# A language-model tower on one core: a Fourier weight update and a weight split moved into the attention, and each stage's first loads into the stage ahead

## The reference

```
h = b_tok + sum over k of Wt[k][context token k]        # k = 0..3: four rows gathered per token
x = layernorm(h)
q, k, v = split(x @ w_qkv.T + b_qkv)                    # 32 query heads, 8 key heads of 32 channels
q, k = rope(q), rope(k)
s = q k^T / sqrt(32), causal;  o = softmax(s) v         # four query heads share one key head
h = h + o @ w_o.T + b_o
x = layernorm(h)
base = x @ W_base.T + b_base
e = x @ enc.T                                           # enc: 40 x 1024
update = sum over 3 experts of irfft((e @ (coefs*mask).T) as Fourier coefficients)
h = h + base + 0.5 * update
```

## Time and profile before

| | us |
|---|---|
| runs, median of 3 | 3591.53 (3586.33 to 3592.12) |
| profiled execution | 3592.34 |
| its span | 3590.5 |
| granted clock, mean | 0.973 |

### The profile page before, as it was taken

The page is one execution under the profiler, slowest core; times in us unless marked ns, Lnnn a source line. Parts: engine busy times, 40 slices in busy tenths (PEclk is TensorE's granted clock), DMA queues, the critical chain, the costliest instruction groups (busy, mean ns, idle before and its releaser), DMA issues. The chain is left out here.

```text
span 3590.5 us, 62180 instructions
## 1 busy us (share of the span) xinstructions
PE 3407.1 (95%) x25088; PEld 2360.7 (66%) x25088; DVE 2269.7 (63%) x3912; ACT 1413.4 (39%) x1660; POOL 2236.0 (62%) x1029
## 2 busy tenths in 40 slices
PE   1999999899999999999999999999996699999999
PEld 1778888656666666666666666666663388888887
DVE  3577776677777677777767777776770444444443
ACT  2222232145555555555555555555554210011110
POOL 4443220068989998998999899899887022222222
PEclk8999999789999999999999999999998699999999
DMA  9999873412122112212212221221111533334432
GB/s 234 246 249 233 234 208 115 121 35 50 38 62 53 41 48 58 51 38 62 53 41 49 58 51 37 63 54 40 49 31 52 181 72 92 93 93 93 93 93 65
DMA packets 245886, 325.90 MB, mean 91 GB/s; under 512 B 64090, under 2 KB 153818, under 8 KB 245634
## 3 DMA queue, kind: packets, MB, share of 16 engines
q1 hardware_dynamic: 227202, 255.29, 26.5%
q0 software_dynamic: 18432, 67.12, 8.8%
HBM read 223.74 MB, written 97.52 MB: 89 GB/s over the span
## 5 line engine op out<-in xcount | busy, mean ns | idle before, releaser
L742 DVE TENSOR_REDUCE mpart<-mx_ps 128x1 f32<-128x512 f32 (+3 forms) x2560 | 1432.7, 605 | 519.3 <-PE mx_ps L795 338.5
L711 ACT ACTIVATE probs<-st_ps 128x1024 f32<-128x1024 f32 (+1 forms) x1152 | 1063.8, 974 | 852.3 <-PE st_ps L826 621.1
L792 PE MATMUL mx_ps<-k_max,qs 96*128 96x512 f32 (+3 forms) x2560 | 908.5, 416 | 19.9 <-POOL masks L660 17.0
L826 PE MATMUL st_ps<-qs,k_score 98*128 98x512 f32 (+1 forms) x2304 | 723.2, 408 | 0.2
L685 POOL TENSOR_TENSOR sums<-probs 128x1024 f32<-128x1024 f32 x256 | 609.5, 2381 | 161.4 <-ACT probs L711 161.3
L792 PEld LDWEIGHTS mx_ps<-k_max,qs 96*128 96x128 f32 x2560 | 467.7, 195 | 297.1 <-DVE mpart L742 188.9
L687 POOL TENSOR_TENSOR sums<-sums,probs 128x1024 f32<-128x1024 f32 x256 | 608.8, 2378 | 25.5 <-ACT probs L711 6.9
L844 PE MATMUL od_ps<-probs,vs 128*32 128x256 f32 (+1 forms) x9216 | 592.1, 375 | 0.0
L693 POOL TENSOR_TENSOR sums<-sums,probs 128x1024 f32<-128x1024 f32 (+1 forms) x256 | 538.7, 2104 | 20.4 <-ACT probs L711 0.4
L826 PEld LDWEIGHTS st_ps<-qs,k_score 98*128 98x128 f32 x2304 | 421.3, 194 | 72.5 <-ACT probs L711 11.9
L1058 POOL TENSOR_TENSOR h<-h,bb 128x1024 f32<-128x1024 f32 x32 | 105.1, 3283 | 542.8 <-DVE xn_c L1156 542.8
(11 more groups left out here) (104 smaller groups left out, 4006.2 us busy)
## 6 DMA issues: line engine op xcount, KB each, us to landing
qs<-q_hi_scratch SPq DMA_DIRECT2D x128, 256.0 KB, 4.6
h_scratch<-hbuf SPq DMA_DIRECT2D x32, 512.0 KB, 8.4
q_hi_scratch<-rot_hi SPq DMA_DIRECT2D x64, 256.0 KB, 3.5
q_lo_scratch<-rot_lo SPq DMA_DIRECT2D x64, 256.0 KB, 4.2
qs<-q_lo_scratch SPq DMA_DIRECT2D x64, 256.0 KB, 5.7
o_scratch<-od_sb SPq DMA_DIRECT2D x128, 128.0 KB
o_in<-o_scratch SPq DMA_DIRECT2D x32, 512.0 KB, 4.5
o_in<-recip_scratch SPq DMA_DIRECT2D x128, 128.0 KB, 7.7
```

The costliest lines, as they stand in the source:

```text
L711: nc.scalar.activation(probs[:, n % SLOTS, half, :, lo:QW], st_ps[:, half, :, lo:QW], ACT.Exp, scale=float(HD) ** -0.5).then_inc(exp_done, 1)
L742: nc.vector.tensor_reduce(mpart[:, h * TPC + t, kc:kc + 1], mx_ps[:, e % MAX_BANKS, 0:w], AX, ALU.max).then_inc(max_done, 1)
L792: mm = nc.tensor.matmul(out, qs[c][0:K_ROWS, h, t * P:(t + 1) * P], k_max[0:K_ROWS, kc * CT:kc * CT + w], start=True, stop=not diagonal)
L826: mm = nc.tensor.matmul(out[:, :, lo:QW], k_score[0:M_ROW + 2, kt * P:(kt + 1) * P], qs[c // 2][0:M_ROW + 2, h:h + 2, at + lo:at + QW], st ...
```

## The change

1. A class `Handover` holds the buffers and semaphores that two stages share: B's first operands, the coefficients, the Fourier slabs and the base weight, C's first operands and two slabs of w1.
2. **In stage A.** Ahead of the last chunk's stores, SP issues 30 loads: two column blocks of the first group's queries, its keys for the maxima, four constants, the coefficients and masks, two Fourier slabs. POOL, done gathering, casts the masks and makes `wr`. SP no longer waits at A's end for the rotated and value stores; B does, on SP and POOL, where they are read.
3. **At B's start.** `FIRST_LEAD` is 14: 66 entries. After entry 8 and every third from there stands a product of a Fourier slab (eight), after entry 36 and every third a delta product (eight). ACT scales `tw` and copies each delta to SBUF, POOL adds it to the base weight, SP stores w1 to DRAM. The first scores wait until ACT has taken all deltas.
4. **In groups 2 to 9 of B**, one slab of the output weight each: SP loads it, ACT rounds it in two halves (steps 8 and 10), DVE subtracts in two halves (steps 12 and 14). Both parts stay in SBUF for stage C. In group 12 DVE inverts the first sequence's denominators in eight parts.
5. **In the last group** SP loads C's first two attention results with their reciprocals and two slabs of w1. B no longer waits for its last stores; C does.
6. **Stage C** starts with tile 0's attention product, then tile 1's in a PSUM place of its own, while w1's eight slabs are read back and split: three before tile 0 is normalised, five after. The second sequence's denominators are inverted in tile 1. The loops are written out.

```diff
-LEAD, FIRST_LEAD = 18, 12
+LEAD, FIRST_LEAD = 18, 14
+FOUR_AT, DELTA_AT = 8, 36
+W_O_GROUP, DEN_GROUP, DEN_PARTS = 2, 11, 8
+W_IN, EARLY_W1 = 3, 3
 # part_a, SP
+            def attention_operands():
+                sp.wait_ge(tr_ready, TILES)
+                for s in range(2):
+                    sp.wait_ge(rot_stored[s], 16 * LAST * QK_TILES)
+                load_queries(sp, hand, q_hi, q_lo, 0, 0)
+                load_keys(sp, hand.k_max, (k_hi, k_lo, k_hi), 0, 0, hand.k_max_loaded)
...
             for n in range(CHUNKS):
+                if n == LAST:
+                    attention_operands()
...
-                sp.wait_ge(v_stored[t], 16 * CHUNKS)
-            for s in range(2):
-                sp.wait_ge(rot_stored[s], 16 * CHUNKS * QK_TILES)
 # part_a, POOL
+            pool.wait_ge(hand.masks_in, 64)
+            nc.gpsimd.tensor_copy(hand.masks[:], hand.consts_in[:]).then_inc(hand.masks_done, 1)
+            cf, mkf, wr, step = hand.cf, hand.mkf, hand.wr, Steps(pool, hand.prep, 0)
+            pool.wait_ge(hand.coefs_in, 16 * 2 * E)
+            step.do(nc.gpsimd.tensor_copy(mkf[:], mk8))
+            step.do(nc.gpsimd.tensor_tensor(cf[:], cf[:], mkf[:], ALU.mult))
...
 # part_b, POOL
+            for c in range(DC):
+                pool.wait_ge(base_in[c], 16)
+                pool.wait_ge(delta_taken, c + 1)
+                nc.gpsimd.tensor_tensor(hand.base[:, c, :], hand.base[:, c, :], hand.four[c][:], ALU.add
+                                        ).then_inc(w1_ready, 1)
 # part_b, ACT
+            def weight_high(c, n):
+                cols = slice(n * 512, (n + 1) * 512)
+                act.wait_ge(w_raw_in, 16 * (c + 1))
+                nc.scalar.copy(w0_hi[:, c, cols], w_raw[:, cols]).then_inc(w0_hi_done, 1)
...
+            act.wait_ge(tw_ready, DC)
+            nc.scalar.activation(tw[:], slot_ps[0][0:R, :], ACT.Identity, scale=SCALING).then_inc(tw_done, 1)
+            for c in range(DC):
+                act.wait_ge(delta_ready, c + 1)
+                nc.scalar.copy(hand.four[c][:], slot_ps[(c + 1) % 2]).then_inc(delta_taken, 1)
 # part_b, DVE
+            def weight_low(c, n):
+                cols = slice(n * 512, (n + 1) * 512)
+                dve.wait_ge(w0_hi_done, 2 * c + n + 1)
+                nc.vector.tensor_tensor(w0_lo[:, c, cols], w_raw[:, cols], w0_hi[:, c, cols].bitcast(F32), ALU.subtract
+                                        ).then_inc(w0_lo_done, 1)
 # part_b, PE
+            def fourier(c):
+                if c == 0:
+                    pe.wait_ge(hand.prep, 4)
+                pe.wait_ge(four_in[c], 16)
+                for n in range(2):
+                    mm = nc.tensor.matmul(slot_ps[0][0:R, n * 512:(n + 1) * 512], hand.wr[:, c, :],
+                                          hand.four[c][:, n * 512:(n + 1) * 512], start=(c == 0), stop=(c == DC - 1))
+                mm.then_inc(tw_ready, 1)
+            def delta(c):
+                if c == 0:
+                    pe.wait_ge(enc_in, 16)
+                    pe.wait_ge(tw_done, 1)
+                if c >= 2:
+                    pe.wait_ge(delta_taken, c - 1)
+                for n in range(2):
+                    mm = nc.tensor.matmul(slot_ps[(c + 1) % 2][:, n * 512:(n + 1) * 512], enc_sb[:, c * P:(c + 1) * P],
+                                          tw[:, n * 512:(n + 1) * 512], start=True, stop=True)
+                mm.then_inc(delta_ready, 1)
+            upfront = [n for k in range(FIRST_LEAD) for n in AT_STEP[k]]
+            for j, n in enumerate(upfront):
+                give(0, n)
+                for what, at in ((fourier, FOUR_AT), (delta, DELTA_AT)):
+                    c, between = divmod(j - at, 3)
+                    if between == 0 and 0 <= c < DC:
+                        what(c)
             groups(group)
 # part_c, PE
+            attention_out(0)
+            attention_out(1)
+            turn_x(0)
+            pe.wait_ge(w_lo_done, DC)
+            last_layer(0)
+            turn_x(1)
+            for t in range(2, TILES):
+                attention_out(t)
+                last_layer(t - 1)
+                turn_x(t)
             last_layer(TILES - 1)
 # part_c, ACT
+            a_high(0)
+            for c in range(EARLY_W1):
+                weight_high(c)
+            a_high(1)
+            for t in range(TILES):
+                act.wait_ge(var_ready, t + 1)
+                nc.scalar.activation(std[:], var[:], ACT.Sqrt).then_inc(std_ready, 1)
+                if t == 0:
+                    for c in range(EARLY_W1, DC):
+                        weight_high(c)
+                elif t + 1 < TILES:
+                    a_high(t + 1)
+                x_high(t)
```

More of the change, by code:

```diff
@@ L35 @@
 R = R0 + R1
+SBUF_BYTES = 212832
 SCALING = 16.0 / 32.0
@@ L1020, in _, with load_o @@
-            sp.wait_ge(tw_ps_done, DC)
-            sp.wait_ge(recip_stored, 16)
-            load_o(0, 0)
-            load_h(0, 0)
-            for n in range(DC, NW):
-                load_w(n)
-            sp.wait_ge(delta_ready, DC)
-            load_o(1, 1)
-            sp.wait_ge(w_lo_done, NW)
-            load_h(1, 1)
-            def tile(t, s, first, last):
-                if not last:
+            def load_o(t):
+                if t == QT:
+                    sp.wait_ge(recip_stored, 32)
+                load_attended(sp, hand, o_dram, recip_dram, t)
@@ new lines, in _ @@
+            load_w1(2)
+            load_h(1)
+            sp.dma_start(bb[:], b_base.rearrange("(a d) -> a d", a=1).broadcast_to([P, D])).then_inc(bb_in, 16)
+            for c in range(W_IN, 6):
+                load_w1(c)
+            for s in range(2):
+                sp.wait_ge(stored[s], B_STORES)
+            parts = lambda a: a[HEADS:2 * HEADS].rearrange("h (a t) -> (h a) t", a=P // HEADS)
+            sp.dma_start(den[:], parts(den_dram)).then_inc(den_loaded, 16)
+            sp.wait_ge(a_ready, 1)
@@ L1169, in _ @@
-            finish(TILES - 1, 1)
+            attended(1)
+            for c in range(EARLY_W1):
+                weight_low(c)
+            a_low(1)
+            for t in range(TILES):
+                normalised(t)
+                if t == 0:
+                    for c in range(EARLY_W1, DC):
+                        weight_low(c)
+                elif t + 1 < TILES:
+                    attended(t + 1)
+                    a_low(t + 1)
+                if t >= 1:
+                    finished(t - 1)
+                x_low(t)
+                if t == 1:
+                    dve.wait_ge(den_loaded, 16)
+                    nc.vector.reciprocal(den[:], den[:]).then_inc(den_inverted, 1)
@@ L1171, in _ @@
+            finished(TILES - 1)
         @block.tensor
         def _(pe):
[L1173 to L1181 removed]
@@ L1194, in turn_x, with attention_out @@
+            def attention_out(t):
+                pe.wait_ge(a_lo_done, t + 1)
+                if t >= 2:
+                    pe.wait_ge(h1_done, t)
+                product(out_ps(t), (a_hi, a_lo), 0).then_inc(o_ready, 1)
+            def turn_x(t):
                 pe.wait_ge(xn_ready, t + 1)
-                if not first:
+                if t >= 1:
                     pe.wait_ge(x_lo_done, t)
```

517 lines of the change are left out of this document (273 added, 244 removed).

## The result

The changed kernel takes 3564.7 us in the median of four runs (3562.2 to 3567.7) against 3591.8 (3586.3 to 3594.8) on the same chip: ratio 0.9926, 95% interval 0.9914 to 0.9937. It is faster by 27 us where 51 were forecast. The time lies 2.7 us above the upper end of the range. The profiled run took 3567.1 us for a span of 3565.3. A second series on another chip gave 3565.6 (ratio 0.9922, 0.9908 to 0.9935).

What follows compares the result with a forecast made beforehand. PE was taken to bound the kernel inside B, with idle handovers between stages. From 3590.5: -14.4 start of B, +38.6 front block, -3 first group, +5 output weight, -76.7 stage C gave 3540.0 us of span, 3541 measured; range 3510 to 3562.

Steps and rivals of the forecast that it cites:

- Start of B: Handover from stage A to B: the first maximum comes 14.4 us sooner, bounds 11.3 and 14.9.
- Front block: B's opening 66 entries with 16 Fourier and delta products: 71.8 us, 38.6 more than before; 20.6 more with deltas high.
- the rest of the first group: What follows the front block in B: nine maxima fewer, 0.3 us each, so -3 us.
- Output weight in B: Groups 2 to 9: 16 subtractions on DVE, 0.65 us each; PE loses 0.3 each, +5 us; bounds nothing to 48.
- the likeliest case: The forecast's own case, deltas at the low clock: 54%, 3541 us, own range 3530 to 3552.
- The rule that I named: DVE instructions with two SBUF inputs and GpSimd ones reading SBUF exclude each other: 1.2 us waiting per subtraction, 19 us uncovered.
- Stage C: Last-layer product starts 39.3 us after the attention's last sum, 116.0 before: gain 76.7 us, bounds 72 and 80.
- nothing in the rest of C is longer: After the first last-layer product: the added reciprocal, half of one of 6.55 us, fits beside tiles of some 22 us.
- the +2 of the sum: Early stage C: one or two meetings of POOL's and DVE's adds lengthen the work before the last-layer product by 2 us.
- high in the deltas: Rival, front block of B: the clock stays high through the delta products, -18 us, 3523; chance 30%.
- rise in the Fourier blocks: Rival, front block of B: the clock does not rise in the Fourier blocks either, +15.6 us, 3557; chance 10%.
- The starving subtractions: Rival, groups 2 to 9: each of 16 waits up to 6.9 us for POOL's sums, 104 us for 5, 3640; chance 6%.

## Why the prediction was wrong

Its sum was 3540.0 us of span; 3565.3 came. Point by point:

- **Start of B** (-14.4): -13.9. Right, and SP's 30 loads ahead of the last stores cost PE 0.6 us at most (last value product 673.58 against 672.99).
- **Front block** (71.8 us): 75.3. The clock came out as I took it in the main, high in the Fourier blocks and low in the deltas, though it was still high for the first entries (0.86 from 675 to 680), where I took low: 3.0 us to the first Fourier product (3.4 forecast), 25.7 to the first delta (25.7), 46.7 from there to the first scores (42.7). The miss is mostly the delta product's price, 3.78 us in place of the 3.41 taken from the earlier trace rows. Against it the rest of the first group made up 7.5 us, not 3.
- **Output weight in B** (+5): +26. This is the step that failed, at the words "three banks cover about one maximum: 0.3 us each". I took the subtraction nearly at its own 0.65 us and let DVE's idle 33 us per group pay for it. DVE's idle time is short pieces between maxima; an operation of 2.42 us at step 12 and one of 2.77 at step 14 stop row maxima that PE needs within 1.0 and 2.0 us. PE lost the difference, 1.4 and 0.8 us, 1.1 for each in the mean, and in six groups 1.5 us more to the clock, which the prediction had in no term. Its bounds for the term reached from nothing to 48 us, so the mechanism was named; the value inside them was wrong, and the likeliest case's range took in little of what lay above it. The rule that I named and then priced at a quarter of itself, the Trainium skill, "SBUF — State Buffer", "Who interferes with whom", gave +19: the measured wait, 1.94 us each (2.59 less the 0.65 of the sum), was longer than the 1.2 worked out from it, as both subtractions came just behind a sum's start. The Trainium skill's statement on that page, "Summary: rules for kernel authors", that the later one waits until the first has finished agrees with the ends of the rows above.
- **Stage C** (-76.7, last-layer product at 39.3): 38.1. Right. Its sentence "nothing in the rest of C is longer" was wrong by 6.5 us: 1.9 for a first product at a partly low clock (12.76 against 10.89), 3.0 at attention product 3, and 1.6 for a last product at low clock. I had looked at whether DVE has time for the reciprocal, not at who waits for its result nor at the load that they need behind it. POOL's adds lengthened DVE's low parts ahead of the first last-layer product by 4.1 us (four in 9.04, 1.23 each alone), twice the +2 of the sum, and still that product started 1.2 us sooner than forecast.
- **The rivals.** The clock was not high in the deltas; it did rise in the Fourier blocks. The starving subtractions were the right place and the wrong price: DVE got in after one sum each time, so 26 us and not 104.

The misses: 21 in the output weight, 5 in stage C, 3.5 in the front block less 4.5 in the first group. Without the first the forecast would have been within 5 us, in part by luck, as the last two cancel.

Open: why the pause at step 12 drops the clock in the third to the eighth of these groups and not in the first two, in both series alike. It isn't the groups themselves: in the kernel with 128 rows, whose groups begin some 15 us sooner, the first seven take 129.8 to 129.9 us and the eighth 128.3. And open is what in a product of 40 rows keeps the clock at its lower level. The share of the array that the stationary operand fills can't be it alone, as the Fourier products fill as much (128 by 40 against 40 by 128) and ran at 1.00. No kernel with a row count in between was run for these products; the attention's maxima and scores, of 96 and 98 rows in the reduced type, run at 1.00 for most of stage B.

## What to carry to other kernels

An engine's idle time is worth only its longest unbroken piece: before an operation is laid among others, compare its length, with the longest wait that a neighbour can add, with the time until the critical engine needs the next result. A DVE operation with two SBUF operands beside a stream of POOL operations took up to one POOL operation longer here (1.03 to 2.77 us for 0.55 of its own, beside sums of 2.38); give it one operand, give it to POOL, or put it where a POOL operation is about to end or where the next need is far. Matmuls over few rows deserve a look at the granted clock: padding the operands with zeros made these twice as fast.

## What the runs showed that I had not expected

- Zero rows make a product faster: 40 rows 3.78 us at a granted clock of 0.50, 128 rows 1.9 us at 1.00, the same columns. The whole kernel gains 18.6 us by it, by the medians.
- The wait for POOL's operation is exact (ends within 0.03 us of each other over eight groups), and the other side pays as well: the sum that follows a subtraction of 512 columns takes 2.68 to 2.84 us in place of 2.38, behind one of 256 columns 2.41 to 2.58.
- A pause of PE of 1.1 us in a stream that is otherwise full was followed by most of 4 us at the lower clock in six of eight groups, 1.5 us of time each; behind one 0.25 us shorter the clock never fell.
